# One-pass products of split features in the matrix hops, plain attribute gathers, moved end buffers

## The chip, the cores and the metric

The kernel runs on one core of a Trainium2 chip. The metric is the time of one execution on the device, in microseconds (us). A core has a matrix engine (TensorE, PE in the profile; its weight loads are PEld), a vector engine (DVE), a scalar engine (ACT), GpSimd (POOL) and SyncE (SP), which issues transfers. The transfers of all of them run on 16 DMA engines. Matrix products accumulate in eight PSUM banks of 128 by 512 fp32.

## What is computed

Four graph layers run one after the other on 3125 nodes of 256 features and 50000 edges; after each comes a residual and a layer normalization:

```python
x = _layernorm(x + L0(x))      # two transformer layers: edge softmax, FFN
x = _layernorm(x + L1(x))      # four-head edge attention
x = _layernorm(x + L2(x))      # two hypergraph convolutions
x = _layernorm(x + L3(x))      # messages from node rows and edge attributes

def _hconv(x, W, b, src, dst, n):                       # layer L2, twice
    xt = x @ W
    m   = segment_sum(xt[src], dst, num_segments=n) * Binv[:, None]
    out = segment_sum(m[dst],  src, num_segments=n) * Dinv[:, None]
    return out + b
```

The change is about layer L2, and about the edge attributes and the buffers of layer L3. Everything is fp32, and the edges arrive sorted by `dst`.

## The kernel before

The nodes are padded to 25 windows of 128 rows (`W = 25`). Layer L2 does not gather edges. The earlier stages count, for every pair of nodes, the edges between them, in a 3200 by 3200 table in device memory (`AT`) and its transpose (`AM`). Each of the four segment sums of L2 is then a product of the count matrix with the features: a **hop**. `h0` and `h2` go from `XS` (features times W1 or W2) with `AT` to `MEAN`; `h1` and `h3` go from `MEAN` with `AM` to `HX`.

A hop has five **parts** of five windows each. For a part, SP loads 25 blocks of 128 by 640 counts (320 KB each, one per source window `u`) into a ring of `RIGHT` buffers, `LEFT`. PE multiplies each block, 128 columns at a time as weights, with the 256 features of window `u`, into five PSUM banks, one per target window (`hop_products`). At the end of a part DVE scales the banks (`hop`), and after `h1` and `h3` goes on with `end2`: PReLU, and after `h3` residual and layer norm.

PE's first stage (`a0`) goes window by window: `turn_a` transposes the normalized window, ACT copies it, `project_a` multiplies it by W1 into a bank, ACT copies that to `XS` (`table_copy`), and PE does the products of part 0 of `h0` for that window. In the same stretch DVE ends the layer before (`end1`, cut in pieces by `Ahead`) and waits for ACT's exponentials and square roots. The projections for `h2` lie between the products of `h1`, and those for L3 (`turn_l3`, `project_l3`, whose results go to the table `YT`) between the products of `h3`.

POOL issues the indirect transfers in one fixed order: the gathers of layer L1, 416 gathers of edge attributes (`ATTR`, 4 numbers per edge, added on to zeros in `PA`), and 416 gathers of `YT` rows for L3, which wait for the whole table `YT`. The order of work on each engine is that of the code; engines wait on semaphores. In the tile names of the profile nearly all of SBUF is one tensor, `arena`.

Of the kernel before, what the change touches and what calls it, by code (L numbers as in the profile page):

```python
# [6 lines left out]
BF = mybir.dt.bfloat16  # L7
ALU = mybir.AluOpType
# [3 lines left out]
NN = 3125  # L12
# [29 lines left out]
RIGHT = 5  # L42
# [64 lines left out]
def program(nc, a, out):  # L107
# [7 lines left out]
    arena = nc.alloc_sbuf_tensor("arena", [128, ARENA], F)  # L115
# [7 lines left out]
    def view(o, *dims):  # L123
        n = int(np.prod(dims))
        ap = arena[:, o:o + n]
        if len(dims) == 1:
            return ap
        names = "abcd"[:len(dims)]
        return ap.rearrange("p (%s) -> p %s" % (" ".join(names), " ".join(names)),
                            **{names[i]: dims[i] for i in range(len(dims))})  # L130

# [108 lines left out]
    WA = WM[:, 0:512].rearrange("p (k n) -> p k n", k=2)  # L240
    WB = WM[:, 512:1024].rearrange("p (k n) -> p k n", k=2)
    b1_, b2_ = WM[:, 1024:1280], WM[:, 1280:1536]
    W0 = WM[:, 0:128]
    W1c = WM[:, 128:256]
# [31 lines left out]
    gbn = misc(4).rearrange("p (j k) -> p j k", k=2)  # L276
    T2 = view(o_q + 3328, T, 2)
# [16 lines left out]
    XS, MEAN = view(o_acc, W, 256), view(o_q, W, 256)  # L294
    LEFT = view(o_w + 1536, RIGHT, 640)

# [5 lines left out]
    HX = view(o_S, W, 256)  # L302
    PT = view(o_ring + 3400, 2, 5, 256)
    XT3 = view(o_ring, 2, 512)
    YB = view(o_ring + 1024, 4, 512)

    Y3 = view(o_w + 256, 5, 4, 512)
    assert o_w + 256 + 5 * 2048 <= o_wv + 2240
    SCALED = [view(o, 4, 4, 128) for o in (o_S, o_S + 2048, o_S + 4096, o_q)]
    OH3 = view(o_q + 2048, 3, 512)  # L310
# [90 lines left out]
    elu_exp = Signal(nc, "elu_exp", a0=5)  # L401
    left_used = Signal(nc, "left_used", **{h: 5 * (W - 1) for h in HOPS})
# [34 lines left out]
    gen_in = Signal(nc, "gen_in", gen=7)  # L437
    gen_sums = Signal(nc, "gen_sums", gen=7, keys=1)
    gen_used = Signal(nc, "gen_used", gen=7)
    gen_place = Signal(nc, "gen_place", gen=2, keys=1, counts=1)  # L440
    compared = Signal(nc, "compared", gen=KG)
    krow_in = [Landed(nc, f"krow_in{k}") for k in range(3)]
    keys_out, gen_counted = Landed(nc, "keys_out"), [Landed(nc, f"gen_counted{k}") for k in range(4)]
    gen_zeros, gen_back = Landed(nc, "gen_zeros"), Landed(nc, "gen_back")
    gen_put = [Landed(nc, f"gen_put{k}") for k in range(KS)]

    W_LOADS = dict(layer0=14, ffn0=16, qkv1=24, layer1=30, ffn1=32, l1=36, l2=41, l3=45)
# [48 lines left out]
    def sync_engine():  # L496
# [40 lines left out]
        with SY.If_ne(unsorted, 0):  # L537
            for k in range(KS):
                SY.dma_start(flat(tg1[k], C)[:, 0:1564], zero[:, 0:1564]).then_inc(gen_zeros.sem, 16)
                SY.dma_start(flat(tg1[k], C)[:, 1564:C * 8], zero[:, 0:1564]).then_inc(gen_zeros.sem, 16)  # L540
                for h in range(4):
                    SY.dma_start(flat(tg2[k], T)[:, 832 * h:832 * (h + 1)], zero[:, 0:832]).then_inc(gen_zeros.sem, 16)
# [148 lines left out]

        def load_sources(i):
# [28 lines left out]
        load_w(WA, kview(a["L2_gnn_W1"]))  # L721
        load_w(WB, kview(a["L2_gnn_W2"]))
        load_w(b1_, rows_bc(a["L2_gnn_b1"], 256))
        load_w(b2_, rows_bc(a["L2_gnn_b2"], 256))
        load_w(a_bc, a["L2_gnn_a"].rearrange("(o k) -> o k", o=1).to_broadcast([128, 1]))
        n = 0
        for h, name in enumerate(HOPS):
            if h == 1:
                for k in range(4):
                    SY.wait_ge(*am_out[k](2 * W))  # L730
                SY.wait_ge(*taken("a0", W))
                load_w(W0[0:64, 0:64], a["L3_gnn_w_00_0"])
                load_w(W0[0:64, 64:128], a["L3_gnn_w_01_1"])
                load_w(W1c[0:64, 0:64], a["L3_gnn_w_10_1"])
                load_w(W1c[0:64, 64:128], a["L3_gnn_w_11_0"])
            for part in range(5):
                for u in range(W):
                    if n >= RIGHT:
                        SY.wait_ge(*left_read(n - RIGHT))
                    SY.dma_start(LEFT[:, n % RIGHT, :],  # L740
# [18 lines left out]
    def pool_engine():  # L759
# [72 lines left out]
        with GP.If_ne(unsorted, 0):  # L832
            GP.wait_ge(*gen_zeros(24))
# [1752 lines left out]
```

## Time and profile before

| | |
|---|---|
| time, median of 3 runs | 5620.3 us (5606.59 to 5629.95) |
| span of the profiled execution | 5234.5 us |
| median less span | 385.8 us |
| PE, PEld, DVE, ACT, POOL busy | 76%, 59%, 52%, 35%, 71% |
| mean granted TensorE clock | 0.891 of full speed |

The profile gives the span of its execution and no other time of it; the third row is its distance to the median of the runs. PE's busy time is the union of its matrix instructions. The shares are means over stages that have different limits. The program goes through L0 (to about 2830 us), L1 (to 3424), L2 (3424 to 4640) and L3.

### The profile page before, as it was taken

The numbers are of one execution on the slowest core, as the hardware profiler recorded it, in microseconds if no ns is written. First come the engines' busy times: TensorE is split into PE (matmuls) and PEld (weight loads), VectorE is DVE, ScalarE is ACT, GpSimd is POOL, SyncE is SP. The second block draws the span as 40 slices with busy tenths as digits, with TensorE's granted clock in tenths as the row PEclk, the third lists the DMA queues.
The fourth block names the chain that finished last, engine by engine and source line by source line (L and its number), as shares of the span: only waits on it lengthen the run. The fifth ranks groups of instructions, "written<-read, shape, count | busy, mean of one in ns | idle before, by whom it ended". The sixth has DMA issues, their size and how long they took to land.

```text
span 5234.5 us, 64530 instructions
## 1 busy us (share of the span) xinstructions
PE 3992.0 (76%) x17691; PEld 3086.9 (59%) x17691; DVE 2746.1 (52%) x6371; ACT 1847.6 (35%) x5458; POOL 3710.0 (71%) x3085
## 2 busy tenths in 40 slices
PE   4565554667985655699796777789999999988886
PEld 3443343445664433466464444468888888877886
DVE  6476667885436555888532888850010002235555
ACT  1154444663334444577232222120000000046665
POOL 4477778888887777888888777788888800037775
PEclk8878777998987777799897888889999999989998
DMA  8699995663339999576423777746666655557676
GB/s 261 200 328 334 329 324 131 161 161 45 31 56 338 338 337 312 132 168 144 75 21 54 208 211 207 178 89 154 153 141 139 149 152 151 153 146 198 198 200 164
DMA packets 734961, 951.33 MB, mean 182 GB/s; under 512 B 277381, under 2 KB 526260, under 8 KB 734472
## 3 DMA queue, kind: packets, MB, share of 16 engines
q1 hardware_dynamic: 419634, 538.30, 34.0%
q0 software_dynamic: 298192, 385.84, 31.5%
q10 hardware_dynamic: 16774, 23.00, 1.2%
q8 instruction: 149, 2.44, 0.2%
q14 instruction: 212, 1.74, 0.1%
HBM read 727.03 MB, written 219.80 MB: 181 GB/s over the span
## 4 chain that ended last, share of the span: by engine, by line
POOL 36%; PE 23%; issue 19%; DMA 16%; SPq 3%; DVE 2%; POOLq 0%; ACT 0%; DVEq 0%
POOL arena L863 24%; PE bank L2443 21%; POOL ATT L900 6%; POOL sc L886 6%; DMA sc<-arena 4%; DMA ATT<-arena 4%; DMA VE<-arena 4%; DMA arena<-KVT,arena 3%; SPq L574 2%; DMA arena<-X1T,arena 1%; PE bank L2152 1%; SPq L570 1%; PE bank L2477 1%; DVE arena L1027 0%; PE bank L2428 0%
## 5 line engine op out<-in xcount | busy, mean ns | idle before, releaser
L2443 PE MATMUL bank<-arena 128*128 128x256 f32 x5000 | 1101.8, 380 | 1.7 <-DVE arena L1686 1.2
L2443 PEld LDWEIGHTS bank<-arena 128*128 128x128 f32 x5000 | 945.5, 190 | 131.4 <-DVE arena L1686 2.0
L863 POOL DMA_INDIRECT arena<-KVT,arena x832 | 808.6, 972 | 278.2 <-issue 239.9
L2287 PE MATMUL bank<-arena 128*128 128x264 f32 x1664 | 606.0, 529 | 453.8 <-ACT arena L1892 439.4
L863 POOL DMA_INDIRECT arena<-YT,arena x416 | 422.9, 1017 | 568.6 <-DMA YT<-arena 442.1
L2287 PEld LDWEIGHTS bank<-arena 128*128 128x128 f32 x1664 | 419.8, 264 | 639.3 <-issue 546.8
L916 POOL DMA_INDIRECT arena<-ATTR,arena x416 | 655.4, 1575 | 144.9 <-issue 144.9
L900 POOL DMA_INDIRECT ATT<-arena x391 | 642.0, 1642 | 130.6 <-issue 110.6
L886 POOL DMA_INDIRECT sc<-arena x391 | 642.5, 1643 | 123.8 <-issue 111.9
L2244 PE MATMUL bank<-arena 128*128 128x273 f32 x1664 | 455.3, 412 | 141.1 <-DVE arena L1406 117.9
L863 POOL DMA_INDIRECT arena<-X1T,arena x416 | 420.4, 1011 | 126.9 <-issue 123.2
L1347 DVE TENSOR_TENSOR arena<-arena,bank 128x256 f32<-128x256 f32 x832 | 292.7, 413 | 375.0 <-DMA arena<-KVT,arena 370.4
L2244 PEld LDWEIGHTS bank<-arena 128*128 128x128 f32 x1664 | 294.6, 191 | 261.5 <-DVE arena L1406 163.5
L2076 ACT ACTIVATE arena<-arena 128x128 f32<-128x128 f32 x1248 | 375.8, 387 | 174.0 <-DVE arena L1233 173.5
L1245 DVE TENSOR_TENSOR arena<-arena,bank 128x273 f32 x832 | 363.4, 437 | 115.0 <-DVE arena L1245 102.2
L2428 PE MATMUL bank<-arena 128*128 128x261 f32 x832 | 292.4, 491 | 140.7 <-DVE arena L1257 140.7
L1883 ACT ACTIVATE arena<-arena 128x264 f32 x832 | 282.9, 411 | 237.9 <-PE bank L2287 155.6
L2536 PEld LDWEIGHTS bank<-arena 128*128 128x128 f32 x2496 | 346.6, 193 | 22.0
L2536 PE MATMUL bank<-arena 128*128 128x128 f32 x2496 | 347.9, 276 | 0.0
L2152 PE MATMUL bank<-arena 128*128 128x256 f32 (+1 forms) x1200 | 312.7, 403 | 38.3 <-ACT arena L1838 22.5
L1892 ACT ACTIVATE arena<-bank,arena 128x8 f32<-128x8 f32 x832 | 208.5, 265 | 362.9 <-DVE arena L1347 331.2
L1913 ACT ACTIVATE arena<-arena 128x128 f32<-128x128 f32 x832 | 265.8, 390 | 192.8 <-PE bank L2244 192.6
(309 smaller groups left out, 5462.0 us busy)
## 6 DMA issues: line engine op xcount, KB each, us to landing
VE<-arena SPq DMA_DIRECT2D x208, 512.0 KB, 5.8
arena<-VE SPq DMA_DIRECT2D x208, 512.0 KB, 3.6
arena<-ATT SPq DMA_DIRECT2D x250, 320.0 KB, 3.0
arena<-AM SPq DMA_DIRECT2D x250, 320.0 KB, 2.9
ATT<-arena POOLq DMA_DIRECT2D x25, 1600.0 KB, 6.6
arena<-LOCT SPq DMA_DIRECT2D x312, 128.0 KB, 5.4
arena<-ATT SPq DMA_DIRECT2D x75, 384.0 KB, 4.3
AM<-arena SPq DMA_DIRECT2D x100, 256.0 KB
```

Of the source, the lines that this page charges most:

```text
L863: GP.indirect_dma_start(out=ring[:, i % n, k, :], out_offset=None, in_=table, in_offset=bass.IndirectOffsetOnAxis(ap=idx[:, 4 * i + k:4 * ...
L886: GP.indirect_dma_start(out=tg3[k], out_offset=bass.IndirectOffsetOnAxis(ap=poss[:, c:c + 1], axis=0), in_=code[:, c:c + 2], in_offset=Non ...
L900: GP.indirect_dma_start(out=ATT, out_offset=bass.IndirectOffsetOnAxis(ap=PLACE[:, c:c + 1], axis=0), in_=ones[:, 0:1], in_offset=None, bou ...
L916: GP.indirect_dma_start(out=PA[:, c, 2:6], out_offset=None, in_=ATTR, in_offset=bass.IndirectOffsetOnAxis(ap=PA[:, c, 0:1].bitcast(I), axi ...
L1245: V.tensor_tensor(dst, dst, bank[banks[k]][:, 0:273].unsqueeze(1), ALU.add).then_inc(added.sem, 1)
L1347: V.tensor_tensor(rows[:, k, :], rows[:, k, :], bank[(4 * i + k) % 8][:, 0:256], ALU.mult).then_inc(qk.sem, 1)
L2076: ins = S.activation(SCALED[i % 4][:, k, c, :], OH3[:, i % 3, 128 * k:128 * (k + 1)], ACT.Copy, scale=PA[:, 4 * i + k, 2 + c:3 + c])
L2152: mm = P.matmul(b_[:, 0:cols], xt[:, k * 128:(k + 1) * 128], wt[:, k, :], start=(k == 0), stop=(k == 1))
L2244: mm = P.matmul(bank[banks[k]][:, 0:r.shape[-1]], oh[:, k * 128:(k + 1) * 128], r, start=True, stop=True)
L2287: mm = P.matmul(b_[:, 0:264], OHQ[:, i % 3, k * 128:(k + 1) * 128], QS[:, i % 4, k, :], start=True, stop=True)
L2443: mm = P.matmul(bank[j][:, 0:256], left[:, 128 * j:128 * (j + 1)], right[:, u, :], start=(u == 0), stop=(u == W - 1))
L2536: mm = P.matmul(s4[:, 0:m + 1:m], by[:, m, :], r8[:, m + 3:8:4 - m], start=False, stop=(m == 3), skip_group_check=True)
```

## The change

An fp32 product of before takes the array several passes. The hops now use the type `float32r` (`FR`) instead, in which an operand is read with a shortened mantissa. Counts are exact in it. Each feature is written as a rounded part, which ACT or DVE make by writing the type, and the rest, which DVE gets by subtracting (`low_part`, and the last step of `mean_of`). The two stand side by side as 512 columns of `XS` and `MEAN`, so that a product streams 512 columns instead of 256, once. DVE adds the two halves of each bank while it scales.

Counts above the exact range would be wrong, so edges that occur that often are taken out into padding rows in the branch for unsorted edges. That branch is not run here, but PE forms the padding rows in each hop with 25 products more (`pick_pads`, with one-hot weights that DVE writes in `pick`). The banks now rotate: part `n` uses five from `(5 n) % 8` on, and the other three serve turns and projections. At a part's start PE does the first three target windows of two blocks before it waits for DVE to have read the banks of the other two. `RIGHT` goes from 5 to 6.

The attribute gathers lose their `compute_op` and `bounds_check`, and `PA` is no longer zeroed for them. The buffers of L2's end and of L3 (`HX`, `Y3`, `SCALED`, `OH3`, `ACC3`, `YB`, `XT3`) lie elsewhere, and the nine weight loads of L2 and L3 are issued before the loads of L1's edges.

```diff
-RIGHT = 5
+RIGHT = 6
+    XS, MEAN = exact("xs", o_q, W, 512), exact("mean", o_S, W, 512)
+    LEFT = exact("left", o_left, RIGHT, 640)
+    def sum_bank(n, j):
+        return bank[(5 * n + j) % 8]
+    def side_bank(n, i):
+        return bank[(5 * n + 5 + i) % 8]
+    def proj_place(r, w):
+        return side_bank(6 + w // 5 if r else 0, 1)[:, 0:256]
...
             GP.indirect_dma_start(
                 out=PA[:, c, 2:6], out_offset=None, in_=ATTR,
-                in_offset=bass.IndirectOffsetOnAxis(ap=PA[:, c, 0:1].bitcast(I), axis=0), bounds_check=R1 - 1,
-                compute_op=ALU.add).then_inc(attr_back.sem, 16)
+                in_offset=bass.IndirectOffsetOnAxis(ap=PA[:, c, 0:1].bitcast(I), axis=0)).then_inc(attr_back.sem, 16)
...
+        def low_part(r, w):
+            V.wait_ge(*right_made(f"a{r}", w + 1))
+            V.tensor_tensor(XS[:, w, 256:512], proj_place(r, w), XS[:, w, 0:256].bitcast(F),
+                            ALU.subtract).then_inc(taken.sem, 1)
+        def mean_of(h, part):
+            name, n = HOPS[h], 5 * h + part
+            for js in ((0, 1), (2, 3), (4,)):
+                ws = [5 * part + j for j in js]
+                for j, w in zip(js, ws):
+                    V.wait_ge(*hop_sum(name, w + 1))
+                    d.mark(V.tensor_scalar(TT[:, j % 2, :], sum_bank(n, j)[:, 0:256], IN_DEG[:, w:w + 1], None, ALU.mult))
+                d.settle()
+                for j, w in zip(js, ws):
+                    V.scalar_tensor_tensor(MF[:, j, :], sum_bank(n, j)[:, 256:512], IN_DEG[:, w:w + 1], TT[:, j % 2, :], ALU.mult,
                                            ALU.add).then_inc(hop_out.sem, 1)
+                V.wait_ge(*hop_out(name, ws[-1] + 1))
+                for j, w in zip(js, ws):
+                    d.mark(V.tensor_copy(MEAN[:, w, 0:256], MF[:, j, :]))
+                d.settle()
+                for j, w in zip(js, ws):
+                    V.tensor_tensor(MEAN[:, w, 256:512], MF[:, j, :], MEAN[:, w, 0:256].bitcast(F),
+                                    ALU.subtract).then_inc(mean_made.sem, 1)
...
-        for w in range(1, W):
+        for w in range(W):
             get.upto(w)
+            if w >= 2:
+                low_part(0, w - 2)
+            pick(0, w)
...
-                mm = P.matmul(bank[j][:, 0:256], left[:, 128 * j:128 * (j + 1)], right[:, u, :],
+            for j in js:
+                mm = P.matmul(sum_bank(n // W, j)[:, :], left[:, 128 * j:128 * (j + 1)], right[:, u, :],
                               start=(u == 0), stop=(u == W - 1))
...
+        def pick_pads(h, u):
...
+            P.matmul(side_bank(5 * h, 2)[:, :], PICKL if u == W - 1 else PICK[:, m % 4, :], right[:, u, :],
+                     start=(u == 0), stop=(u == W - 1)).then_inc(pick_used.sem, 1)
...
+            for u in range(2):
+                hop_products(h, part, u, range(3))
+            P.wait_ge(*hop_out(was, done + 1))
+            P.wait_ge(*hop_out(was, done + 2))
+            for u in range(2):
+                hop_products(h, part, u, range(3, 5))
```

PE in the first stage before, one window (`L2157` is the transpose, `L2152` the projection, `L2443` a hop's product):

```order
L2157 MATMUL bank<-arena 128x128 [waits copied,ready]
L2157 MATMUL bank<-arena 128x128
L2152 MATMUL bank<-arena 128x256 [waits taken,copied]
L2152 MATMUL bank<-arena 128x256
L2443 MATMUL bank<-arena 128x256 [waits left_in1,taken]
L2443 MATMUL bank<-arena 128x256 x4
```

The same window now (`L2360`, `L2355`, `L2650`, and `L2665` for the padding rows):

```order
L2360 MATMUL bank<-arena 128x128 [waits copied,ready]
L2360 MATMUL bank<-arena 128x128
L2355 MATMUL bank<-arena 128x256 [waits taken,copied]
L2355 MATMUL bank<-arena 128x256
L2650 MATMUL bank<-xs,left 128x512 [waits taken,left_in5]
L2650 MATMUL bank<-xs,left 128x512 x4
L2665 MATMUL bank<-xs,pick 128x512 [waits taken,pick_made]
```

One product is added per window, and `taken`, which ACT's copy gave before, now comes from DVE's subtraction.

DVE in that stage before (`L1663` is the last step of the ELU, `L1543` to `L1160` the layer norm of five windows):

```order
L1663 SCALAR_TENSOR_TENSOR arena<-arena 128x1280 [waits elu_exp,dve_steps]
L1543 BN_STATS arena<-arena 128x6 [waits dve_steps]
L1543 BN_STATS arena<-arena 128x6 x4
L1548 BN_AGGR arena<-arena 128x2 [waits dve_steps]
L1548 BN_AGGR arena<-arena 128x2 x3
L1550 BN_AGGR arena<-arena 128x2
L1553 RECIPROCAL arena<-arena 128x5 [waits root]
```

The same piece now (`L1810` is `low_part`, `L1805` is `pick`):

```order
L1782 SCALAR_TENSOR_TENSOR arena<-arena 128x1280 [waits elu_exp]
L1662 BN_STATS arena<-arena 128x6 [waits dve_steps]
L1662 BN_STATS arena<-arena 128x6 x4
L1810 TENSOR_TENSOR xs<-bank,xs 128x256 [waits right_made]
L1805 TENSOR_SCALAR pick<-arena 128x12
L1667 BN_AGGR arena<-arena 128x2 [waits dve_steps]
L1667 BN_AGGR arena<-arena 128x2 x3
L1669 BN_AGGR arena<-arena 128x2
L1672 RECIPROCAL arena<-arena 128x5 [waits root]
L1810 TENSOR_TENSOR xs<-bank,xs 128x256 [waits right_made,dve_steps]
```

DVE's steps for PE's current windows now stand between its steps for the next part, and each waits for ACT's copy of a projection.

## Rows read from the trace of the kernel before

**Rows 1.** The page: span, and chain that ended last by line.

```profile
span 5234.5 us, 64530 instructions
...
POOL arena L863 24%; PE bank L2443 21%; POOL ATT L900 6%; POOL sc L886 6%; DMA sc<-arena 4%; DMA ATT<-arena 4%; DMA VE<-arena 4%; DMA arena<-KVT,arena 3%; SPq L574 2%; DMA arena<-X1T,arena 1%; PE bank L2152 1%; SPq L570 1%; PE bank L2477 1%; DVE arena L1027 0%; PE bank L2428 0%
```

**Rows 2.** Windows, each engine's busy time by stage.

```profile
core 0: us, PE busy (x) PEld busy (x) DVE busy (x) ACT busy (x) POOL busy (x), PEclk, DMA share, GB/s
2860.00:3400.00 540.00, 401.88 (x1829) 266.24 (x1827) 436.89 (x1307) 118.69 (x404) 414.95 (x411) 0.86 0.76 204
3436.00:3522.00 86.00, 80.93 (x382) 69.66 (x383) 48.95 (x113) 35.00 (x66) 71.40 (x44) 0.93 0.42 86
3522.00:4614.00 1092.00, 1090.27 (x5154) 952.78 (x5154) 98.01 (x195) 41.57 (x94) 554.82 (x356) 1.00 0.60 148
4310.00:4614.00 304.00, 303.42 (x1487) 261.38 (x1486) 54.03 (x112) 22.16 (x43) 0.00 (x0) 1.00 0.51 148
4614.00:4644.00 30.00, 16.16 (x67) 12.38 (x65) 15.96 (x32) 9.34 (x21) 0.30 (x1) 0.58 0.14 53
```

**Rows 3.** Chain that ended last, three pieces of it: start, us, what.

```profile
4051.29 4.32 PE bank L2443 x20
...
4613.69 2.22 DVE arena L1680 x5
...
5195.30 0.67 PE bank L2536 x6
```

**Rows 4.** Groups by line and form, 3522 to 4614 us.

```profile
L2443 PE MATMUL bank<-arena 128*128 128x256 f32 x4764 | 1046.1, 380 | 1.7 <-DVE arena L1686 1.2 <-DVE arena L1680 0.6
L2443 PEld LDWEIGHTS bank<-arena 128*128 128x128 f32 x4764 | 899.8, 190 | 124.9 <-DVE arena L1686 2.0 <-DVE arena L1680 1.0
...
L1686 DVE TENSOR_SCALAR arena<-bank,arena 128x256 f32<-128x256 f32 x50 | 21.9, 483 | 493.5 <-PE bank L2443 493.5
```

**Rows 5.** Timeline of PE, one window's period in the first stage.

```profile
3473.20 2.32 PE L2443 MATMUL bank<-arena 128*128 128x256 f32 x10
3475.36 0.38 PE L2157 MATMUL bank<-arena 128*128 128x128 f32 x2
...
3476.45 0.81 PE L2443 MATMUL bank<-arena 128*128 128x256 f32 x3
```

**Rows 6.** DMA queues, 3600 to 4100 us: packets, MB, share of 16 engines.

```profile
q1 hardware_dynamic: 31724, 71.54, 51.4%
q0 software_dynamic: 37254, 0.55, 11.6%
...
arena<-ATTR,arena POOLq DMA_INDIRECT x260
```

**Rows 7.** DMA queues, 1600 to 1700 us, the most loaded stretch.

```profile
DMA packets 19862, 34.14 MB, mean 341 GB/s; under 512 B 1917, under 2 KB 14748, under 8 KB 19855
```

**Rows 8.** Costliest groups of the page, POOL's two kinds of indirect transfer.

```profile
L916 POOL DMA_INDIRECT arena<-ATTR,arena x416 | 655.4, 1575 | 144.9 <-issue 144.9
...
L863 POOL DMA_INDIRECT arena<-X1T,arena x416 | 420.4, 1011 | 126.9 <-issue 123.2
```

**Rows 9.** Timeline of POOL, attribute gathers' ends and what follows.

```profile
3401.66 1.59 POOL L916 DMA_INDIRECT arena<-ATTR,arena  x1 [0.30 <-issue]
...
4200.04 1.55 POOL L916 DMA_INDIRECT arena<-ATTR,arena  x1 [0.31 <-issue]
4643.70 1.01 POOL L863 DMA_INDIRECT arena<-YT,arena  x1 [442.12 <-DMA YT<-arena]
```

**Rows 10.** Timeline of DVE, one part of five windows in the first stage.

```profile
3467.67 1.69 DVE L1651 TENSOR_TENSOR arena<-arena 128x320 f32<-128x320 f32 x4
...
3476.47 1.49 DVE L1663 SCALAR_TENSOR_TENSOR arena<-arena 128x1280 f32<-128x1280 f32 x1 [2.47 <-ACT arena L2013]
...
3481.92 0.19 DVE L1553 RECIPROCAL arena<-arena 128x5 f32<-128x5 f32 x1 [1.70 <-ACT arena L1818]
...
3483.88 1.69 DVE L1651 TENSOR_TENSOR arena<-arena 128x320 f32<-128x320 f32 x4
```

More of the change, by code:

```diff
@@ new lines, in vector_engine @@
+            for j in range(HOT):
+                V.tensor_reduce(rmax, hot_k_, AX, ALU.max).then_inc(gen_in.sem, 1)
+                V.wait_ge(*gen_sums("hots", 2 * j + 1))
+                V.tensor_reduce(top_k[0:1], bank[5][0:1, 0:128], AX, ALU.max).then_inc(gen_in.sem, 1)
+                V.wait_ge(*gen_sums("hots", 2 * j + 2))
+                d.mark(V.tensor_copy(hot_keys[:, j:j + 1], bank[5][:, 128:129]))
+                d.then(V.tensor_scalar(hot_t_, hot_k_, 1.0, None, ALU.add))
+                d.then(V.scalar_tensor_tensor(hot_k_, hot_k_, hot_keys[:, j:j + 1], hot_t_, ALU.is_lt, ALU.mult))
+                d.then(V.tensor_scalar(hot_k_, hot_k_, -1.0, None, ALU.add))
@@ new lines, in rest @@
+            def rest():
+                d.then(V.scalar_tensor_tensor(hot_d, hot_s, -float(NP), hot_keys, ALU.mult, ALU.add))
+            d.then(V.tensor_scalar(hot_s, hot_keys, 1.0 / NP, None, ALU.mult))
+            d.then(V.tensor_copy(hot_si, hot_s))
+            d.then(V.tensor_copy(hot_s, hot_si))
+            rest()
+            d.then(V.tensor_scalar(hot_m, hot_d, float(NP), None, ALU.is_ge))
+            d.then(V.tensor_tensor(hot_s, hot_s, hot_m, ALU.add))
+            rest()
+            d.then(V.tensor_scalar(hot_m, hot_d, 0.0, None, ALU.is_lt))
@@ new lines, in vector_engine @@
+            d.then(V.tensor_tensor(hot_s, hot_s, hot_m, ALU.subtract))
+            rest()
+            d.then(V.tensor_scalar(hot_u, hot_keys, 0.0, None, ALU.is_ge))
+            for dst, x in ((HOTS, hot_s), (HOTD, hot_d)):
+                d.then(V.scalar_tensor_tensor(dst, x, 1.0, hot_u, ALU.add, ALU.mult))
+                d.then(V.tensor_scalar(dst, dst, -1.0, None, ALU.add))
+            for k, x in enumerate((hot_keys, HOTS, HOTD)):
+                d.then(V.scalar_tensor_tensor(hot_m, x, 1.0, ident[:, 0:HOT], ALU.add, ALU.mult))
+                d.then(V.tensor_reduce(hot_c[:, k:k + 1], hot_m, AX, ALU.add))
@@ L2147, in tensor_engine @@
             mm.then_inc(gen_sums.sem, 1)
+            for j in range(HOT):
+                P.wait_ge(*gen_in("hots", 2 * j + 1))
+                P.transpose(bank[5][0:1, 0:128], rmax, ident).then_inc(gen_sums.sem, 1)
+                P.wait_ge(*gen_in("hots", 2 * j + 2))
+                P.matmul(bank[5][:, 128:129], ones[0:1, :], top_k[0:1], start=True, stop=True).then_inc(gen_sums.sem, 1)
         P.end_ifs()
```

393 lines of the change are left out of this document (269 added, 124 removed).

## The prediction

> **What bounds the kernel now.** I read the page's chain of waits by line first, then the windows by stage, then the pieces of the chain in the hops. The chain names two costs above the others: POOL's gathers, and one line of PE, L2443, the products of the hops, with 21% of the span [rows 1]. In the windows the hop stretch from 3522 to 4614 us is 1092 us long, PE is busy for 1090.3 of them at a granted clock of 1.00, and DVE and ACT are nearly idle [rows 2]. It is a pure PE stretch. In the chain 20 records of L2443 take 4.32 us [rows 3], two records to a product, so a product of 256 columns lasts 0.432 us. 19 parts of 125 products are 2375 x 0.432 = 1026 us; another 27 are the 25 turns and projections for `h2` (1.09 us each, 3475.36 to 3476.45 [rows 5]); the other 39 are L3's turns and projections and short waits at hop ends.
>
> After the hops comes a tail of 30 us (DVE, then PE, ACT and the last `YT` write), and then L3, which POOL's gathers pace: 421.7 us busy of 548 in the window [rows 2], and the first one starts when `YT` is there, at 4643.70 [rows 9].
>
> **The products.** The change keeps the number of products and streams 512 columns once. 0.432 us for 256 columns at 2.4 GHz is 4.05 column times for each column (256 columns once are 0.1067 us at 2.4 GHz, the upper of the clock's two levels). At one pass 512 columns take 0.213 us. With the 2.5 ns by which each record exceeds its columns now (0.216 against 0.2133) it is 0.216 us. The trace has no record of this type, so the bounds: not below 0.213; above, two passes, 0.43. I take 0.216, since the operand is no longer expanded into parts, which is all that makes two records out of one product.
>
> Weights: each product now needs one load where it needed two. Between two products of 256 columns a load hides wholly (0.216 us per record with loads of 0.190 [rows 4]), and in L3 six records of 128 columns with six loads follow each other in 0.67 us [rows 3], 0.112 per load. So one load hides under 0.213 us; if it did not hide at all, a product would last 0.190 + 0.213 = 0.403.
>
> PE's work in the stretch is then 1092 - 1026 + 513 (2375 x 0.216) + 16 (75 padding products outside the first stage) = 595 us. At the ends of parts PE has nine products, 1.9 us, between the first window's sum and its wait for two windows of DVE. DVE needs four readings of a bank at 0.483 us [rows 4], 1.9 us. That cancels, and the hop ends' full waits of about 1 us go: 591 us. DVE's new readings, copies and subtractions (some 8 us per part) lie under 27 us of products.
>
> **The loads.** They hid under 5 x 0.432 = 2.16 us per block. Now a block lasts 1.08 us on PE. From 3600 to 4100 us q1 moved 71.54 MB, which is 218 blocks of 0.3277 MB, with 51.4% of 16 engines' time: 0.514 x 500 / 218 = 1.18 us of all engines per block. That is more than 1.08, so by the busy share the loads would bound. But the share overstates what a transfer costs when the engines are lightly used: 0.60 of the engines' time for 148 GB/s in the hops, gathers included [rows 2], would mean a ceiling of 247 GB/s, and the fullest stretch of the trace moved 341 [rows 7]. At 341 a block costs 0.96 us and hides. The attribute gathers compete for the first part of it: 0.116 x 500 / 260 = 0.223 us of all engines each [rows 6]. With one every 1.25 us (below) they take up to 18%, which leaves 1.18 / 0.82 = 1.43 us per block from 3530 to 3922: 274 blocks. The other 201 blocks at 1.18 us and about 14 us of `YT` writes are 251. Slow end: 392 + 251 = 643 us. Fast end: PE's 591. I take the middle, 617, as neither price is measured at this load: the stretch falls from 1092 to 617, **475 us less**.
>
> The Trainium skill (DMA: Bandwidth & Descriptors, its opening table) gives about 358 GB/s as a core's limit at device memory. By it a block would cost 0.915 us, the loads would hide, and the stretch would be PE's 591. The 341 GB/s in the trace is close to that limit, but was reached with another mix of transfers, reads and writes on two queues.
>
> **The first stage.** From 3436 to 3522 PE needed 3.25 us per window, 2.16 of them products [rows 5]. Now it needs 1.09 + 1.08 + 0.22 for the padding = 2.39. But DVE's period for five windows, 3467.67 to 3483.88, already was 16.2 us, of which it waited 2.47 and 1.70 for ACT [rows 10], so it worked 12.0. Now come five readings of a bank (0.483 each) and five small one-hot writes (about 0.2): 15.4, and because `low_part` ties DVE to PE's and ACT's current window, I keep the 4.2 of waits: 19.6 us per five windows for the four parts that have work for a next part, against 16.2. That is 14 more; the last five windows run at PE's 2.39, 4 less, and the last two blocks' products 2 less: **+8 us**. Below, the bound is PE's own 25 x 2.39 = 60 instead of 86, 26 less; above, each `low_part` waiting a whole round of PE, ACT and DVE, 1.5 us more per window, +35. The memsets of the one-hot tiles add 1.
>
> **The attributes.** 416 gathers went from 3401.66 to 4201.6 [rows 9]: 1.575 us each and the issue gap. Without `compute_op` the nearest rows are the X1T gathers: 1.011 us each and 123.2 of gaps over 416 [rows 8], 1.31 us. They then end after 520 to 545 us, at 3922 to 3947. The next user, L3's gather, can start at 4643.7 - 475 + 12 = 4181. So this is worth nothing beyond not being in the way: unchanged, the gathers would end at 4202 and cost 21 us.
>
> **The rest.** At the tail DVE reads each bank twice, with waits: 5.2 us instead of 2.2 [rows 3]: **+3**. In L1 nine more small loads on SP are hidden: SP waits there for POOL's count transfers. L3 keeps its instructions, and its places in SBUF change nothing that a row shows: 0.
>
> The sum: -475 + 8 + 1 + 3 = -463. Against the profiled execution: span 5234.5 - 463 = 4771.5 us. The runs' median lies 385.8 us above the span, and I take that distance as fixed: 5620.3 - 463 = **5157 us**.
>
> **Rivals.**
> 1. *The loads bound throughout.* If they get no more than what they have beside the gathers, 1.43 us per block, all the way, the stretch is 475 x 1.43 = 679 us and the time 5219. For it: 0.60 of the engines' time was taken at 148 GB/s; against it: 341 was reached. Chance 0.13.
> 2. *The clock sags.* In L1, where PE is busy 402 of 540 us with short waits, the granted clock is 0.86 [rows 2]. If PE's waits for blocks did that to the hops, 591 / 0.86 = 687 us: 5227. Against it: PE would still be busy for nine tenths. The Trainium skill (TensorE: Matmul & The Clock Gate, A second HAM failure mode: psum-queue depth-cycling) tells of this for products of 512 columns that go round the banks; the trace has the clock at 1.00 with products that go round five banks. Chance 0.05.
> 3. *The new type needs two passes over its 512 columns.* A product then lasts 0.432, as before, and there are 100 more of them. The stretch is 1092 + 75 x 0.432 = 1124, the first stage 11 longer, and with the 12 of above the time is 5620 + 32 + 11 + 12 = 5675, slower by 1%. It decides from 0.42 us per product on: 2450 products plus 62 us equal the old stretch at 0.42. Against it: nothing is left to expand. The Trainium skill (Perfetto Trace Analysis, Engine Utilization) halves the array's rate for one kind of fp32 product; whether this type is one of them, no row shows. Chance 0.04.
> 4. *The weight loads do not hide*: 0.403 per product, 2450 x 0.403 + 62 = 1049, so 5620 - 43 + 12 = 5589. Chance 0.02.
> 5. *Better than forecast*: loads hide (591) and DVE keeps up in the first stage (-26 instead of +8): 5620 - 501 - 26 + 4 = 5097. Chance 0.10.
>
> The forecast itself, 5120 to 5195 (PE's 591, and the slow end of 643, with 10 us for the first stage), has 0.66.
>
> **The numbers.** The range has to leave out at most 2 in 10: rivals 3 and 4 (0.06) lie outside, and a little of 1 and 5. 5095 to 5230. A measurement of this kernel tells 0.5%, 28 us, from no change. Faster by more than that: all but rival 3 and part of rival 4, 0.94; within: 0.02; slower: 0.04.
>
> **What would show it.** Right: hop products with one record each of 128x512, 20 of them in 4.3 us; about 617 us between the first stage and the last product; SP's loads landing in more than the 3 us of now; attribute gathers 1.0 us long and ended near 3950; PE waiting for DVE in the first stage, about 94 us long. Wrong: products spaced by more than 0.22 us at a clock of 1.00 with no wait between them; a clock under 0.95 in the hops; a first stage over 110 us; L3 longer than its 591 us (4643.7 to the end).

## The result: no change that counts, where 8% was forecast

The changed kernel takes 5645.57 us (median of 9 runs, 5623.35 to 5654.52), the kernel before 5622.72 (median of 9, 5606.59 to 5632.91) beside it: a ratio of 1.0036, 95% interval 1.0022 to 1.005. The forecast was 5157.

Executions of both kernels fall into two conditions, each of which held for a whole series of runs and shows in the kernel before alone, which takes some 5235 us in one and 5620 us in the other (below, **the 5235** and **the 5620 condition**). The 5620.3 us that the prediction started from, and the result, are of the 5620 condition; the trace that it read, with its span of 5234.5 us, is of the other.

The windows by stage of the changed kernel, from the profiled execution of the result (span, then the columns of [rows 2]): the gathers for L1, L1's end, the first stage, the rest of the hops, the tail, L3's gathers.

```profile
core 0 of [0], span 5645.4 us
core 0: us, PE busy (x) PEld busy (x) DVE busy (x) ACT busy (x) POOL busy (x), PEclk, DMA share, GB/s
3045.00:3700.00 655.00, 413.68 (x1805) 287.06 (x1805) 437.00 (x1279) 115.51 (x400) 411.53 (x417) 0.79 0.63 168
3700.00:3883.00 183.00, 25.79 (x68) 17.49 (x68) 37.98 (x104) 4.79 (x12) 136.59 (x144) 0.54 0.12 15
3883.00:4320.00 437.00, 101.86 (x299) 72.36 (x300) 61.52 (x162) 35.76 (x67) 280.74 (x274) 0.57 0.11 19
4320.00:4947.00 627.00, 627.00 (x2842) 509.14 (x2840) 198.28 (x489) 44.09 (x97) 0.00 (x0) 1.00 0.82 255
4947.00:4979.00 32.00, 14.80 (x61) 11.49 (x60) 17.65 (x36) 8.98 (x21) 0.45 (x1) 0.55 0.11 42
4979.00:5594.00 615.00, 522.41 (x3203) 471.54 (x3204) 270.72 (x594) 364.07 (x1215) 404.30 (x415) 0.90 0.62 177
```

The hops did what the forecast says: 627 us, PE busy in all of them at a clock of 1.00, at 255 GB/s, where [rows 2] had 1092. But the first stage, forecast at 94 us, takes 437, and the end of L1 ahead of it 183. In these 437 us PE works for 102 and the transfers move 19 GB/s: nobody is busy but POOL, with its gathers.

PE's timeline there (start, duration, engine, line, count, in brackets the idle time before) is regular: a window of the first stage every 33.60 us (32.90 to 34.29 in the nine from 3957 to 4259 us), where [rows 5] had 3.25.

```profile
4057.34 0.66 PE L2360 MATMUL bank<-arena 128*128 128x128 f32 x2 [17.89 <-issue]
4070.84 2.05 PE L2355 MATMUL bank<-arena 128*128 128x256 f32 x4 [12.83 <-issue]
4072.32 2.69 PE L2650 MATMUL bank<-xs,left 128*128 128x512 f32 x5
4074.81 0.63 PE L2665 MATMUL bank<-xs,pick 128*128 128x512 f32 x1
4090.94 0.66 PE L2360 MATMUL bank<-arena 128*128 128x128 f32 x2 [15.50 <-issue]
...
4124.54 0.66 PE L2360 MATMUL bank<-arena 128*128 128x128 f32 x2 [17.39 <-issue]
```

ACT's timeline of the same stretch shows which signal is late. L2293 copies what the turn L2360 leaves in its bank.

```profile
4056.81 0.38 ACT L2293 ACTIVATE arena<-bank 128x256 f32<-128x256 f32 x1 [22.02 <-issue]
4068.01 0.38 ACT L2286 ACTIVATE xs<-bank 128x256 fp32r<-128x256 f32 x1 [10.82 <-remote]
...
4090.41 0.38 ACT L2293 ACTIVATE arena<-bank 128x256 f32<-128x256 f32 x1 [20.41 <-remote]
```

The turn that starts at 4057.34 ends at 4058.00; its copy starts at 4090.41, 32 us later, with ACT idle for 20 of them. PE's next turn then starts 0.15 us after that copy's end. So the signal from ACT to PE is prompt, and the one from PE to ACT is 32 us late. The semaphore updates that the same trace records say so directly: the one for this turn is at 4090.39, and at 4067.99 is the one for a projection that had ended at 4037.45. The same pair in the 5235 condition (the run after_again below) has 0.04 us between the turn's end (3464.03 + 0.38) and the copy:

```profile
3464.03 0.38 PE L2360 MATMUL bank<-arena 128*128 128x128 f32 x2
3464.44 0.38 ACT L2293 ACTIVATE arena<-bank 128x256 f32<-128x256 f32 x1 [1.22 <-PE bank L2360]
```

The stall lies beside the attribute gathers, to the end: they run from 3701.2 to 4256.0. The window that starts at 4258.94 still takes 25.9 us, the one at 4284.85 takes 5.2, and the next part begins at 4320.

```profile
L980 POOL DMA_INDIRECT arena<-ATTR,arena x416: 940/944/1957, 3701.2 to 4256.0; - x139
```

### The profile page after: what moved, and what is told of

The parts are those of the page before. It is cut to its first block, busy times and chain, and to the rows that moved or that the text cites. A ratio compares the mean times of both kernels' runs of the same rounds, so it can differ in the third digit from the quotient of the medians.

```text
span 5645.4 us, 59886 instructions
## 1 busy us (share of the span) xinstructions
PE 3618.7 (64%) x15291; PEld 2680.2 (47%) x15291; DVE 2869.4 (51%) x6725; ACT 1858.3 (33%) x5462; POOL 3438.4 (61%) x3085
## 4 chain that ended last, share of the span: by engine, by line
issue 26%; PE 23%; POOL 19%; DVE 11%; another core or an unknown queue 10%; DMA 6%; SPq 3%; ACT 1%; DVEq 1%; ACTq 0%; POOLq 0%
PE bank L2650 10%; POOL arena L927 6%; POOL sc L950 6%; POOL ATT L964 6%; PE bank L2775 6%; PE bank L2772 4%; DMA ATT<-arena 3%; DMA sc<-arena 2%; SPq L620 2%; DVE arena L1376 2%; DVE arena L1746 2%; DVE arena L1466 2%; DVE arena L1352 1%; PE bank L2490 1%
## 5 line engine op out<-in xcount | busy, mean ns | idle before, releaser
L927 POOL DMA_INDIRECT arena<-YT,arena x416 | 405.7, 975 | 932.6 <-DMA YT<-arena 721.6
L2490 PEld LDWEIGHTS bank<-arena 128*128 128x128 f32 x1664 | 384.9, 248 | 872.8 <-issue 663.6
L2631 PE MATMUL bank<-arena 128*128 128x261 f32 x832 | 315.8, 530 | 293.9 <-DVE arena L1376 158.2
L980 POOL DMA_INDIRECT arena<-ATTR,arena x416 | 416.4, 1001 | 139.7 <-issue 139.7
L2263 ACT ACTIVATE arena<-arena 128x128 f32<-128x128 f32 x1248 | 374.4, 387 | 257.7 <-issue 145.5
L2775 PE MATMUL bank<-arena 128*128 128x128 f32 x2496 | 403.5, 293 | 71.9 <-issue 71.1
L2355 PE MATMUL bank<-arena 128*128 128x256 f32 (+1 forms) x1200 | 326.9, 417 | 176.5 <-issue 102.5
L2775 PEld LDWEIGHTS bank<-arena 128*128 128x128 f32 x2496 | 384.1, 207 | 117.4 <-issue 89.5
L2447 PEld LDWEIGHTS bank<-arena 128*128 128x128 f32 x1664 | 294.8, 192 | 261.7 <-DVE arena L1525 132.4
L2631 PEld LDWEIGHTS bank<-arena 128*128 128x128 f32 x832 | 185.1, 251 | 396.3 <-DVE arena L1746 201.4
L1925 DVE TENSOR_TENSOR arena<-arena,bank 128x256 f32 x416 | 173.5, 417 | 371.3 <-remote 272.9
L2355 PEld LDWEIGHTS bank<-arena 128*128 128x128 f32 x1200 | 239.8, 215 | 221.8 <-issue 142.1
L2360 PE MATMUL bank<-arena 128*128 128x128 f32 x500 | 117.9, 334 | 343.5 <-issue 169.1
```

What stands on the lines that cost most here:

```text
L927: GP.indirect_dma_start(out=ring[:, i % n, k, :], out_offset=None, in_=table, in_offset=bass.IndirectOffsetOnAxis(ap=idx[:, 4 * i + k:4 * ...
L980: GP.indirect_dma_start(out=PA[:, c, 2:6], out_offset=None, in_=ATTR, in_offset=bass.IndirectOffsetOnAxis(ap=PA[:, c, 0:1].bitcast(I), axi ...
L2263: ins = S.activation(SCALED[i % 4][:, k, c, :], OH3[:, i % 3, 128 * k:128 * (k + 1)], ACT.Copy, scale=PA[:, 4 * i + k, 2 + c:3 + c])
L2355: mm = P.matmul(b_[:, 0:cols], xt[:, k * 128:(k + 1) * 128], wt[:, k, :], start=(k == 0), stop=(k == 1))
L2447: mm = P.matmul(bank[banks[k]][:, 0:r.shape[-1]], oh[:, k * 128:(k + 1) * 128], r, start=True, stop=True)
L2490: mm = P.matmul(b_[:, 0:264], OHQ[:, i % 3, k * 128:(k + 1) * 128], QS[:, i % 4, k, :], start=True, stop=True)
```

## The experiments

All but two are single profiled executions. "Before" is the time of the kernel before in the same series.

### 1. Both kernels, each with the other kind of attribute gather

`before_again` is the kernel before. `after_adding` gives the changed kernel accumulating gathers back, `before_plain` gives the kernel before plain ones (the gather's lines the other way; the memset stays).

```diff
-  in_offset=...IndirectOffsetOnAxis(ap=PA[:, c, 0:1]...)).then_inc(attr_back.sem, 16)
+  in_offset=...IndirectOffsetOnAxis(ap=PA[:, c, 0:1]...), bounds_check=R1 - 1,
+  compute_op=ALU.add).then_inc(attr_back.sem, 16)
...
+  d.mark(V.memset(PA[:, :, 2:6], 0.0))
```

> The kernel before, unchanged, for a profile of an execution that takes what the timed runs take (5620 us; the profile shown of it has a span of 5234.5). Theory A (while POOL issues plain gathers back to back, PE's semaphore increments arrive late; this is in every timed run): the span is about 5620, and the 386 us more lie in the four stages of plain gathers (K twice, X1T, YT), about 70 to 110 us in each, with none in the scatters, the attribute gathers or the hops. Theory B (the clock or the transfers were slower throughout): the 386 us are spread over all stages, hops too.

> The changed kernel with the attribute gathers as before (added on to zeros). Theory A (the plain attribute gathers hold up PE's increments and with them the first stage): the first stage falls from 435 us to about 95, the attribute gathers take 770 to 800 us again and end just before L3 could start, and the time is 5645 less 330 to 350, about 5300. Theory C (the first stage's new round through PE, ACT and DVE is slow by itself): the first stage stays above 400 us and the time within 30 us of 5645.

> The kernel before with plain attribute gathers alone. Theory A: PE signals each used block of counts, so while the plain gathers run SP gets new blocks only every 8 to 30 us; the hops stand nearly still for 520 to 560 us and the time is 5620 plus 350 to 500. Theory C: the hops are as before and the time stays at 5620 within 20 us.

Measured, with before at 5231.5: 5241.65, 4830.14 and 5242.0 us. None of the expectations for 5620 could be met, because nothing stalled: this was the 5235 condition, and what was learned is that there are two.

### 2. The changed kernel again, timed

> The changed kernel, unchanged, beside the kernel before on one chip. In the first call before took 5231 us there, not 5620, and plain attribute gathers did not slow it. Theory A' (the delays of PE's increments belong to a condition of the chip in which the result was taken, plain gathers bring them out, and they cost most where a stage needs many signals in turn): where before takes 5230, the first stage takes about 95 us here too and the time is 4770 to 4830. If before takes 5620 on this chip, the time is about 5645 again. Theory C (the changed first stage is slow with plain attribute gathers on any chip): the time is above 5100 though before takes 5230.

Measured: 4790.36 us (4 runs, 4769.75 to 4799.06), before 5238.5 (7 runs, 5230.38 to 5247.13), ratio 0.9132, 0.9104 to 0.916. The condition was again the 5235 one, and there the change saves 448 us; the forecast was 463. Its windows, in the same order as above:

```profile
core 0 of [0], span 4791.2 us
...
2857.00:3406.00 549.00, 396.58 (x1837) 265.80 (x1838) 437.26 (x1309) 117.22 (x404) 422.49 (x416) 0.87 0.76 201
3406.00:3443.00 37.00, 14.25 (x39) 9.52 (x38) 26.78 (x71) 3.71 (x8) 28.16 (x30) 0.59 0.31 58
3443.00:3535.00 92.00, 68.99 (x302) 53.94 (x303) 62.39 (x165) 35.44 (x67) 71.58 (x68) 0.92 0.34 85
3535.00:4169.00 634.00, 629.41 (x2840) 507.66 (x2838) 199.65 (x489) 44.09 (x97) 307.21 (x321) 1.00 0.83 254
4169.00:4200.00 31.00, 14.79 (x60) 11.50 (x60) 17.56 (x35) 8.11 (x18) 0.00 (x0) 0.53 0.12 43
4200.00:4748.00 548.00, 473.93 (x3248) 437.04 (x3249) 273.86 (x606) 373.90 (x1242) 421.41 (x415) 0.99 0.70 198
```

The hops are about as long here as in the 5620 condition (634 and 627; experiment 4 has the 7 us). What differs is L1's end and the first stage (37 and 92 us instead of 183 and 437), and the stages of plain gathers, L1's (549 for 655) and L3's (548 for 615).

### 3. Which gathers, and where

`few_attributes` fetches 8 of the 416 attribute rows per partition and leaves the others zero, so its last layer computes with zeros there. `late_attributes` holds the gathers back until the first hop's part 1. `adding_2` and `before_2` repeat experiment 1.

```diff
# few_attributes
-  for c in range(T):
+  for c in range(8):
...
+  d.mark(V.memset(PA[:, :, 2:6], 0.0))
...
-  V.wait_ge(*attr_back(T))
+  V.wait_ge(*attr_back(8))
...
-  S.wait_ge(*attr_back(T))
+  S.wait_ge(*attr_back(8))
# late_attributes
+  GP.wait_ge(*left_used("h0", W))
   GP.wait_ge(*attr_out(1))
```

> The changed kernel with 8 of its 416 attribute gathers (the other rows of the attributes are set to zero and never fetched, so the last layer computes with zeros there). The executions so far fall into two conditions, told apart by the kernel before: 5235 us or 5620 us. Theory A (the plain attribute gathers stall the first stage, in the 5620 condition only): there 5645 - 340 (first stage 435 to about 95) - 25 (end of the layer ahead) = about 5280 us; in the 5235 condition the first stage stays at 92 to 95 us and only the loads get easier: hops from 636 to about 600, so 4750 to 4790. Theory C (the changed first stage is slow by itself whenever the chip is in the 5620 condition): 5600 or more there. Forecast's term for the loads (the gathers cost the hops up to 52 us): 4740 in the 5235 condition; rival (PE's own 591 already reached): no more than 5 us less than 4790.

> The changed kernel with its plain attribute gathers held back until the first block of part 1 of the first hop, so that none lies beside the first stage. In the 5620 condition, Theory A in its narrow form (only the chain PE-ACT-DVE-PE of the first stage suffers): first stage about 95, hops 630 to 650, 5645 - 340 = about 5300 us. In its wide form (every increment of PE comes late beside plain gathers): the blocks' releases to the load queue come up to 31 us late, six places in the ring are 6.5 us of cover, and the hops lose most of what the first stage wins, 5500 to 5650. In the 5235 condition: 4790 within 10 (the gathers end at about 4090 instead of 3951, both before the last layer's first gather at 4200).

> The changed kernel with accumulating attribute gathers, as in the earlier run of this edit. In the 5235 condition 4830 us again. In the 5620 condition, Theory A (plain gathers stall, accumulating ones don't): 5620 - 448 + 38 = about 5210 to 5250. Theory D (any gather on GpSimd's queue stalls the first stage there): 5600 or more.

> The kernel before. In the 5235 condition 5235 us. In the 5620 condition its trace shows where the 386 us lie: Theory A: in the stretches with plain gathers (first gathers 253 to about 890, second 1650 to 2275, then 2857 to 3510, and the last layer about 615 instead of 548), with none in the hops and the first stage, where only accumulating gathers run. Rival (everything is slower by 7%): the hops at 1170 instead of 1092.

This series was in the 5620 condition (before 5626.58). Measured: few_attributes 5163.22, late_attributes 5690.97, adding_2 5185.92, before_2 5620.8 us.

The windows of before_2 show where the 386 us lie that the prediction took as standing outside the span.

```profile
core 0 of [0], span 5619.6 us
...
3054.00:3702.00 648.00, 422.12 (x1805) 291.88 (x1805) 436.37 (x1277) 115.75 (x400) 413.11 (x417) 0.78 0.64 171
3702.00:3751.00 49.00, 23.32 (x68) 15.80 (x68) 36.46 (x99) 4.77 (x12) 41.22 (x26) 0.63 0.36 55
3751.00:3841.00 90.00, 85.13 (x402) 73.36 (x403) 50.71 (x117) 35.20 (x66) 74.33 (x44) 0.93 0.42 89
3841.00:4930.00 1089.00, 1087.27 (x5139) 949.84 (x5138) 97.50 (x194) 41.38 (x93) 542.35 (x348) 1.00 0.59 148
4930.00:4958.00 28.00, 14.82 (x61) 11.49 (x60) 14.61 (x29) 8.68 (x19) 0.00 (x0) 0.56 0.15 56
4958.00:5574.00 616.00, 514.10 (x3210) 469.88 (x3211) 272.43 (x597) 366.30 (x1218) 404.58 (x416) 0.91 0.63 177
```

First stage, hops and tail, with accumulating gathers beside them, are as long as in the trace of before. The four stages of plain gathers are longer. From first gather to last, the two of `KVT` take 620.5 and 624.9 us for 535 and 523 in before_again, that of `X1T` 647 for 549, that of `YT` 615 for 543. That is 358 of the 379 us between the two spans (5619.6 and 5240.5). The scatters ahead of them, which accumulate, are the same within 7 us.

So accumulating gathers do no harm in the 5620 condition and plain ones do. With them back, the change saves 441 us there too (adding_2). Theory C, a slow first stage by itself, and Theory D, any gather, fall: adding_2 has the new first stage at 92.0 us. few_attributes is within 1 us of adding_2 up to the last product, so beside the hops the accumulating gathers cost nothing; the 23 us between the two spans are L3's wait for the gathers, which end at 4524 where `YT` was there at 4500.

late_attributes settles the wide form. Its first stage is back at 92 us, and the stall moves with the gathers into the first hop, which now gets a block every 14.0 us instead of the 1.15 of five products. PE's timeline:

```profile
3905.68 2.50 PE L2651 MATMUL bank<-xs,left 128*128 128x512 f32 x5 [11.47 <-DMA left<-ATT]
3919.65 2.50 PE L2651 MATMUL bank<-xs,left 128*128 128x512 f32 x5 [11.47 <-DMA left<-ATT]
3933.84 2.50 PE L2651 MATMUL bank<-xs,left 128*128 128x512 f32 x5 [11.69 <-DMA left<-ATT]
3947.67 2.50 PE L2651 MATMUL bank<-xs,left 128*128 128x512 f32 x5 [11.32 <-DMA left<-ATT]
```

PE seems to wait for loads, but the loads wait for PE's `left_used`. SP's timeline from 3900 to 3990 us has seven issued in 84 us:

```profile
3902.73 84.32 SPq L786 DMA_DIRECT2D left<-ATT  x7
```

From the issue at 3916.73 to the products that use the block it takes 2.9 us, so the transfer itself is quick. The same load follows the recorded update of `left_used` by 0.02 us. But by count of blocks the buffer that it fills had its last product at 3864.5, 52 us earlier. For the loads from 3958.73 to 3986.73 the lag is 78 us, near the 84 us that six blocks of 14.0 us make, and the ring lets PE be no further ahead. So the signals do not come a fixed time late: it is as if they stood in a queue that is served at a rate. A block has five weight loads and five products; 14.0 / 10 is 1.40 us per instruction. A window of the first stage has 2 turns, 4 projections, 5 products and a padding product, each with its load: 24 instructions, and 33.60 / 24 is 1.40 again. The rate also fits inside a window: in ACT's rows above, the copy that follows the projection comes 11.20 us after the one that follows the turn, which is 8 instructions, and the next turn's copy 22.40 us later, which is 16. From such a rate a number for another program follows.

### 4. Kind or distance

`checked` leaves the gathers plain and adds the bounds check alone. `spaced` puts a memset on POOL behind each gather. `paced` issues each gather when the one before has landed. `before_plain_2` is before_plain.

```diff
# spaced, behind each gather
+  if c:
+      GP.wait_ge(pool_set.sem, 6 + c)
+  GP.memset(view(o_key, 384), 0.0).then_inc(pool_set.sem, 1)
# paced, ahead of each gather
+  if c:
+      GP.wait_ge(*attr_back(c))
```

> The kernel before with plain attribute gathers instead of accumulating ones. In the 5235 condition 5242 again. In the 5620 condition, Theory A in the form that the last runs gave it (beside the attribute gathers, 1.33 us apart, PE's increments come as if each PE instruction, load or product, took 1.4 us: 24 instructions and 33.6 us per window of the changed first stage, 10 instructions and 14.0 us per block of the hops): the old first stage has 32 instructions per window (4 of turning, 8 of projecting, 10 loads and 10 records of products), so some 45 us per window, and the gathers' 555 us pass with about 12 windows done: 5620 + 450 to 500 = about 6090. Theory C (the changed first stage alone is slow there): 5620 to 5640.

> The changed kernel, its plain attribute gathers given a bounds check but no accumulation: of the two things in which the accumulating gathers differ from the plain ones, one alone. In the 5620 condition: if the bounds check is what spares PE, 5190 with gathers of 1.6 us or of 1.0; if the accumulation (or the slower rate that it brings) is, 5645. In the 5235 condition 4790, and the gathers' length says which of the two costs 0.55 us.

> The changed kernel, plain attribute gathers with a memset of 128x384 on GpSimd behind each, which brings their distance from 1.33 to about 1.8 to 2.0 us, near that of the accumulating ones (1.93). In the 5620 condition: if the rate of the gathers is what counts (at 1.93 apart the queue drains), 5180 to 5220; if their kind is, the first stage stalls through all of their 770 us, 24 instructions x 1.9 per window: 5700 to 5850. In the 5235 condition about 4790 to 4820.

> The changed kernel, plain attribute gathers one at a time: each is issued when the one before it has landed (some 3 us apart by the landings of other small transfers, 1250 us in all). In the 5620 condition: if a backlog of gathers in the queue holds PE up, the first stage is at 95 us and the time is set by the gathers' end (3700 + 1250, then the last layer's 616 + 55: about 5620); if each gather costs PE the same whatever the backlog, the first stage still stretches, to 24 x 3 us per window or less. In the 5235 condition: gathers from 3407 to about 4660, then the last layer: about 5250.

The condition was 5235 (before 5242.43). Measured: 5230.88, 4785.76, 4788.38 and 5302.14 us. The bounds check costs 66 ns per gather (1.010 us for 0.944), so it is the accumulation that makes one 1.55. spaced has the gathers 1.62 us apart and costs nothing. paced has them 3.17 apart, 1314 us in all where 1250 was expected: L3 waits for their end at 4713. It was run in this condition alone, so its question about a backlog of gathers stays unanswered. Its hops last 626.6 us, against 633.8 in after_again: 7 us is what the close plain gathers take from the loads.

### 5. The same three in the 5620 condition

> The kernel before with plain attribute gathers. In the 5620 condition: if the attribute edit alone holds TensorE up (32 instructions of 1.4 us per window of the old first stage, against a window of 3.25 us), 5620 + 450 to 500 = about 6090; if it takes the new stage as well, 5620 to 5640. In the 5235 condition 5235 again.

> The changed kernel, attribute gathers plain but with a bounds check. In the 5235 condition the check made a gather 1.010 us instead of 0.944, at 1.37 us apart, and 4786 us. In the 5620 condition: 5645 if the kind without accumulation is what holds PE up, 5190 if the missing bounds check is.

> The changed kernel, a memset of 128x384 on GpSimd behind each plain attribute gather. In the 5235 condition the gathers were 1.62 us apart and the time 4788. In the 5620 condition: if the distance counts, 5180 to 5230 (above 1.6 us apart PE is free, or nearly so); if the kind counts, PE is held up for all of the 675 us: 5645 + 120 = about 5765.

Before was 5652.88. Measured: 6151.9, 5685.95 and 5202.31 us.

The attribute edit by itself, in the kernel before, costs 499 us. Its first stage has 32 instructions per window, and 32 x 1.40 is 44.80. The turns in PE's timeline:

```profile
4066.27 0.66 PE L2156 MATMUL bank<-arena 128*128 128x128 f32 x2 [29.28 <-issue]
4111.07 0.66 PE L2156 MATMUL bank<-arena 128*128 128x128 f32 x2 [29.49 <-issue]
4155.87 0.66 PE L2156 MATMUL bank<-arena 128*128 128x128 f32 x2 [29.70 <-issue]
```

They are 44.80 us apart. The first stage is 436.9 us long, just as in the result, though a window takes longer: fewer windows pass before the gathers end, and the rest then go at their old pace. The bounds check makes no difference: a window of checked_2 takes 33.6 us. Distance does: spaced_2 has the same plain gathers, 1.63 us apart, and a first stage of 96.3 us. So plain gathers do harm only when they come close, whatever their number. Accumulating ones never came closer than 1.93 us in any run, so whether they would do harm at 1.34 is not shown.

### 6. The spaced version timed, and a shorter distance

spaced_3 is spaced; spaced_short sets 128 columns instead of 384.

> The changed kernel with a memset of 128x384 behind each attribute gather, timed. In the 5235 condition 4788 (ratio 0.914), in the 5620 condition 5200 (ratio 0.921).

> The same with a memset of 128x128 (0.20 us instead of 0.43), so gathers some 1.42 apart instead of 1.62. In the 5620 condition: if TensorE is spared in proportion to the free time between gathers, a part of the 340 us comes back, 5250 to 5450; if there is a sharp point between 1.37 and 1.62, it is either 5200 or 5680. In the 5235 condition 4787.

The condition was 5620. spaced_3 takes 5175.78 us (4 runs, 5170.8 to 5182.09), before 5625.4 (7 runs, 5615.18 to 5640.76), ratio 0.9199, 0.9177 to 0.922. spaced_short takes 5543.77. The attribute gathers of spaced_3 and of spaced_short (min, median and longest ns, first and last start):

```profile
L980 POOL DMA_INDIRECT arena<-ATTR,arena x416: 947/953/2252, 3703.8 to 4374.9; - x139
```

```profile
L980 POOL DMA_INDIRECT arena<-ATTR,arena x416: 947/950/2219, 3702.6 to 4290.5; - x139
```

Over 415 distances that is 1.617 and 1.417 us; the result has 1.337. At 1.417 the delay comes and goes: L1's end takes 101 us and the first stage 195, with turns 2.5 to 13 us apart, the last two 13.5 and 24; and the stall goes on in the hops, 848.7 us instead of 630. It looks as if PE were served a little more slowly than it works, and fell behind by and by. The time lies between the two values that were expected for a sharp point, and above the range for a share in proportion. Since spaced_short too has a memset behind every gather, the memset by itself is not what helps. Somewhere between 1.42 and 1.62 us the harm ends.

The first stage, hops and tail of spaced_3:

```profile
3757.00:3852.00 95.00, 70.33 (x299) 54.36 (x300) 66.45 (x164) 35.49 (x67) 85.75 (x115) 0.90 0.32 81
3852.00:4483.00 631.00, 629.69 (x2843) 507.64 (x2841) 220.74 (x491) 44.18 (x97) 460.41 (x652) 1.00 0.83 255
4483.00:4514.00 31.00, 14.79 (x60) 11.49 (x60) 17.55 (x35) 8.12 (x18) 0.00 (x0) 0.53 0.12 43
```

spaced is the version to keep: 4788 us in the 5235 condition, as fast as the changed kernel, and 5176 in the 5620 one, 470 us faster than it. The version with accumulating gathers has 4830 and 5186, one execution each; the 10 us between it and spaced_3 in the 5620 condition are no more than the four runs of spaced_3 differ among themselves.

## Why the prediction was wrong

**The step that failed** is in the part on the attributes: the plain gathers are "worth nothing beyond not being in the way", so the sum has no term for what they do to PE. That held by their own time, and it is what the trace of before could show, since nothing there waits for them. In the condition in which the kernel is timed they hold up PE's signals. It cost, against before_2, 134 us at L1's end (183.3 for 49.4 from the last `X1T` gather to the first turn) and 347 in the first stage (436.9 for 89.5, to part 1's first product), 481 together. The hops gave 463 back, tail, L3 and the gathers ahead took 7 more. The sum is +26 between the two spans (5645.4 and before_2's 5619.6), and the medians have +23. Of the signs of being wrong that the prediction lists, three showed: products spaced by more than 0.22 us, a first stage over 110 us, and an L3 longer than 591 us (666.9).

**The step that hid it** is the last of the sum: "I take that distance as fixed". 385.8 us were taken as lying outside the span. They lay inside it, in the stages of plain gathers. The profiled execution of the result ends 1.2 us after its span (5646.56 and 5645.4), so the distance itself was the warning: a span 7% shorter than the shortest run is that of an execution unlike the timed ones. Which stages it lay in no row of before could tell; before_2 showed it. No rival covered it; the range ended at 5230 and the chance of slower or same was 0.06.

**The terms, in the condition of the trace** (before, [rows 2], and after_again):

| term | forecast | measured |
|---|---|---|
| all ahead of the last `X1T` gather | 0 | +5.1 (3400.4 to 3405.5) |
| hops after the first stage | -475 | -455 (1089.1 to 633.8) |
| first stage | +8 | +2.3 (89.6 to 91.9) |
| memsets, in L1's end | +1 | +1.4 (36.0 to 37.4) |
| tail | +3 | +3.2 (28.7 to 31.9) |
| L3, from its first gather to the end | 0 | 0 (590.8 and 590.8) |
| span | -463 | -443 (5234.5 to 4791.2) |

- **Products.** 0.216 us was too little. The shape is right, one record of 128x512 (the group of `h1` and `h3` on the page of after_again; its records overlap, so their mean is longer than their spacing):

```profile
L2650 PE MATMUL bank<-mean,left 128*128 128x512 f32 x1250 | 318.9, 404 | 0.0
```

  But PE needs longer from one to the next. In the chain of waits of the result a run of 60 takes 14.05 us: 0.234 each; from start to start they are 0.226 to 0.239 and 0.2305 on average (0.227 in `h0` and `h2`, whose features come from `XS`, 0.234 in `h1` and `h3`, from `MEAN`, and so again in after_again, few_attributes and paced; why is open), where records of 256 columns came every 0.216 with two to a product. 2375 x 0.0145 is 34 us, and 591 + 34 = 625: the 626.4 us of the undisturbed hops.
- **Loads.** Forecast between hidden and bounding. They hide: 626.4 us with 8 gathers, 626.7 with all of them accumulating, 633.8 with plain ones in the 5235 condition. The middle of 591 and 643 came near the measured time by luck: a product that was too cheap made up for loads that were too dear. A block landed 3.6 us after its issue in after_again (3.0 in before), and PE waited for blocks 4.4 us in all of the hops.
- **First stage.** DVE kept up a little better than counted, and the upper bound of +35 was not needed.
- **Attributes.** 1.31 us apart was forecast and 1.31 measured, the last start at 3951 (forecast 3922 to 3947). The value of the edit is 37 us here (69.1 to 31.9 us between the last product and L3's first gather in after_adding and after_again), forecast 21.
- **The rivals.** The clock did not sag: 1.00 in the hops. What the Trainium skill (TensorE: Matmul & The Clock Gate, A second HAM failure mode) tells of 16-bit products of 512 columns that go round the banks did not occur with these. One pass it was: 0.2305 us is under the 0.42 from which rival 3 decides. The reason given for it, that nothing is left to expand, was not tried by itself, nor how many bits the type keeps. The halved rate of the Trainium skill (Perfetto Trace Analysis, Engine Utilization) is not that of this type. Weight loads of 0.188 us hide under the products; whether they make up the 0.0145 was not tried.

**What stays open.** Why PE's signals are held up, and what makes an execution be in one condition or the other. The chip's number does not decide it: the record gives number 8 both for the first series, in the 5235 condition, and for the last, in the 5620 one. Shown are the place (PE's signals; those of ACT and DVE come at once), the rate (1.40 us per PE instruction in three programs) and the distance of gathers that brings it on. That the longer stages of `KVT`, `X1T` and `YT` in the 5620 condition have the same cause is likely, since they too are plain gathers, 1.26 to 1.32 us apart where nothing holds them up; it was not tried. One rival is untested: every execution of the changed kernel and of the experiments, the timed ones too, has a span and a granted clock on record, so something recorded it. A rate that counts weight loads, which update no semaphore in the trace, would also fit a delay in recording TensorE's instructions, so nothing here shows that an execution that is not recorded would stall.

## What to carry to other kernels

Compare the profiled execution's time with the timed runs before adding anything up. If they differ by more than the runs do among themselves, find out which stages would make up the difference before calling it fixed. And price an edit by what its instructions do to others as well as by its own time: the cheaper gather was cheaper in every row, and a small memset between two of them was worth 470 us in the 5620 condition.

## What the hardware showed that was not expected

- Beside plain indirect gathers of 16 bytes per row issued every 1.34 to 1.35 us, in the 5620 condition, TensorE's semaphore signals arrived as if each of its instructions, loads included, took 1.40 us: 33.60 us for 24, 14.0 for 10, 44.80 for 32. At 1.62 us apart, or accumulating and 1.93 to 1.98 apart, there is no such delay; in the 5235 condition there is none at any distance tried (1.31 to 3.17).
- A plain gather of 16 bytes per row takes 0.944 us on GpSimd, with a bounds check 1.010, accumulating with one 1.549.
- Products of rounded fp32 over 512 columns come every 0.2305 us at a clock of 1.00, 17 ns more than their columns.
